# Audio tower block on one core: score sums of the first group moved to TensorE, folded bias in one matmul, other orders

## The chip, the cores and the metric

The program runs on one core of a Trainium2 chip. The metric is the device time of one execution in microseconds. Everything is in float32, or in float32r halves that together hold a float32.

## What is computed

64 signals of 750 samples are cut into 10 overlapping patches (positions) each; a patch is embedded, then one attention block and one feed-forward block follow, each behind a layer norm and with a residual:

```python
idx = arange(0, 750 - 128 + 1, 64)[:, None] + arange(128)       # 10 patches
h = einsum('bnp,dp->bnd', patches, W_tok) + b_tok               # 512 dims
z = layernorm(h); q, k, v = z @ Wq.T, z @ Wk.T, z @ Wv.T        # 16 heads of 32
q, k = rope(q, k)
s = q @ k.T / sqrt(32), causal
heavy = the key with the largest sum of softmax(s) over the queries
p = softmax(s where |i - j| <= 1 or j is heavy)  # causal mask kept
h = h + (p @ v) @ Wo.T
h = h + (silu(z2 @ Wg.T) * (z2 @ Wu.T)) @ Wd.T                  # z2 = layernorm(h), 2048 inner
```

The shape reaching the attention is 64 batches x 10 positions; the attention's sequence is the position, so its score matrices are 10 x 10 for each batch and head.

## The kernel before, in words

640 tokens lie in five tiles of 128 (`QUADRANTS`: four positions of 32 batches each). For attention the batches are in two groups of 32. Within a group a partition is one batch and one of four quarters of the heads (`NQ`), so each partition holds 4 heads x 32 dims = 128 values of a position, and scores are sums over 32 neighbouring values of a row.

Front part, in order on each engine (each engine's order is written out by hand; semaphores tie them):

- TensorE (`block.tensor`, L840 on) embeds the tokens (`embed_tokens` L847, `embed_bias` L851), folds each projection weight with the token weight (`fold_weight`, L886: main part L890, bias L896), and projects patches straight to k, q, v (`project`, L900): matmuls of 32 columns into four partition quarters at once (L912), then the folded bias is added by two identity matmuls, one for its high half (L917) and one for its low half (L919). `spread_scale` (L921) spreads the norm's reciprocal roots. Eighteen projections: for each group k, q, v in parts of 4, 4 and 2 positions.
- VectorE makes the norms (`statistics`, `token_scale`), rotates k and q of the first group out of PSUM (`rotate`), multiplies q row i with keys 0..i (`key_products`, L228) and sums over 32 dims (`scores`, L630); POOL makes the products of rows 5, 7 and 9. Then come softmax (`softmax_in` L637, `softmax_out` L652, with ScalarE's `exponential` between), `heavy_keys` (L664), the mask, a second softmax in two parts, and the value products (`values`, L232; POOL has queries 9 and 8).
- TensorE sums value products over keys by accumulating transposes (`value_sums`, L947), which also turns them; `project_out` (L955) applies Wo, and `transposes` (L935) turns the normalised tile. ScalarE evicts: `embedded`, `folded`, `folded_bias`, `drain`, `hi_attn`, `whole_tokens`.

The feed-forward runs in two passes over 16 blocks of inner dims. The first pass (token tiles 0 and 1, `gate_up_whole` L1013, `down_whole` L1023) begins as soon as these tiles are normalised; the second group's attention runs beside it on VectorE, POOL and ScalarE, an item or two between the products of two blocks (`first_pass`, L761, L463, L1030). The second pass (tiles 2 to 4, `mm3` L204) starts near 185 us. Block i's `down_whole(i - 1)` on TensorE needs VectorE's product of block i - 1 (`gu_prod`), and a block's buffers are shared by two blocks, so an engine that is late by more than a block stops the others.

SP issues all loads: patches, token weights, dims, bias, k weights, constants, q, v and o weights, then the blocks in four slots.

## Time and profile before

| | |
|---|---|
| median of 3 runs | 300.07 us (299.58 to 300.21) |
| profiled execution, own time | 299.39 us |
| its span | 297.2 us |
| TensorE busy | 270.3 us, 91% |
| VectorE busy | 160.2 us, 54% |
| ScalarE busy | 79.3 us, 27% |
| POOL busy | 63.2 us, 21% |
| mean granted clock of TensorE | 0.975 |

The page cuts the span into 40 slices of 7.4 us and prints the busy share of each in tenths:

```profile
PE   3999999418966999999999999999999999999994
DVE  0774887999789496483710535443443333433323
PEclk9999999857999999999999999999999999999999
```

A 9 is 90% or more. TensorE has weak slices at the start and from the eighth to the thirteenth; in the ninth and tenth the granted clock (1.0 is 2.4 GHz) is low too. PE is TensorE's matmuls, PEld its weight loads, DVE VectorE, ACT ScalarE, POOL GpSimd; `issue` is time in which an engine waited for nothing that the profile shows. Busy time is an average over stages with different limits, so the rows further down are read by stage and by time.

### The profile page before, as it was taken

The page shows a single profiled execution, that of the slowest core. Times are in us where ns is not written, and L with a number is a line of the kernel's source. Part 1 is how long each engine was busy: PE and PEld are TensorE (multiplying, and loading weights), DVE is VectorE, ACT ScalarE, POOL GpSimd, SP SyncE. Part 2 cuts the span into 40 slices and gives each one's busy share as a digit, 9 for nine tenths or more (in the row PEclk, how much of TensorE's full clock was granted, in tenths as well). Part 3 has the DMA queues.
Part 4 walks back from the last instruction along what each step waited for, and adds up shares of the span by engine and source line. Part 5 has one row for each costly group of instructions (what it writes and reads, how often), then busy time and mean ns, then how long its engine had stood idle before and what let it go on. Part 6 is the DMA issues. An engine that isn't in the chain of part 4 may idle for free.

```text
span 297.2 us, 4447 instructions
## 1 busy us (share of the span) xinstructions
PE 270.3 (91%) x1715; PEld 209.7 (71%) x1715; DVE 160.2 (54%) x307; ACT 79.3 (27%) x145; POOL 63.2 (21%) x47
## 2 busy tenths in 40 slices
PE   3999999418966999999999999999999999999994
PEld 1555566216455787676786567789999999999993
DVE  0774887999789496483710535443443333433323
ACT  1322053020411010325010202334443334434320
POOL 0124065000241500003600000123233222233210
PEclk9999999857999999999999999999999999999999
DMA  7971130000000353353340321548423244330003
GB/s 236 426 327 46 63 108 4 0 0 0 3 0 1 106 205 105 116 176 144 131 187 2 106 89 25 191 141 306 169 106 106 106 146 154 124 106 0 0 0 106
DMA packets 6814, 32.44 MB, mean 109 GB/s; under 512 B 976, under 2 KB 976, under 8 KB 6288
## 3 DMA queue, kind: packets, MB, share of 16 engines
q1 hardware_dynamic: 6512, 31.85, 30.6%
q10 hardware_dynamic: 288, 0.39, 0.4%
q8 instruction: 10, 0.16, 0.2%
q14 instruction: 4, 0.03, 0.0%
HBM read 30.93 MB, written 1.31 MB: 108 GB/s over the span
## 4 chain that ended last, share of the span: by engine, by line
PE 77%; issue 10%; DVE 6%; POOL 4%; DMA 1%; ACT 0%; SPq 0%; DVEq 0%; POOLq 0%
PE ps L204 34%; PE ps L1013 16%; PE ps L1023 9%; PE ps L890 4%; PE ps L955 3%; PE ps L947 3%; PE ps L847 2%; POOL prod L228 2%; PE ps L912 2%; DVE prod L228 1%; DMA wtok<-w_tok 1%; DVE by_sin L593 1%; PE ps L896 1%; DVE sm L630 1%; POOL prod L232 1%
## 5 line engine op out<-in xcount | busy, mean ns | idle before, releaser
L204 PE MATMUL ps<-xT,wgu 128*128 128x384 f32 x384 | 70.9, 340 | 0.1
L204 PEld LDWEIGHTS ps<-xT,wgu 128*128 128x128 f32 x384 | 68.1, 188 | 2.5 <-DVE xT L571 0.9
L1013 PE MATMUL ps<-whole,stage 128*128 128x256 f32 (+1 forms) x288 | 58.3, 357 | 1.4 <-ACT whole L368 1.4
L1013 PEld LDWEIGHTS ps<-whole,stage 128*128 128x128 f32 x288 | 49.6, 190 | 12.2 <-issue 3.6
L758 DVE TENSOR_TENSOR gu<-silu,ps 128x256 f32<-128x256 f32 (+1 forms) x32 | 15.5, 486 | 78.3 <-PE ps L204 44.5
L297 POOL TENSOR_TENSOR wd<-stage,wd 128x512 fp32r<-128x512 f32 x16 | 27.1, 1692 | 78.4 <-ACT wd L368 78.4
L461 ACT ACTIVATE silu<-ps 128x256 f32<-128x256 f32 (+1 forms) x32 | 14.0, 437 | 85.0 <-PE ps L1013 58.6
L204 PE MATMUL ps<-wd,hT 128*128 128x512 f32 x144 | 35.7, 393 | 0.0
L1023 PE MATMUL ps<-stage,gu 128*128 128x512 f32 x64 | 30.1, 593 | 2.9 <-DVE gu L758 2.9
L204 PEld LDWEIGHTS ps<-wd,hT 128*128 128x128 f32 x144 | 26.8, 188 | 5.0
L368 ACT ACTIVATE wgu<-stage 128x1024 fp32r<-128x1024 f32 x16 | 16.9, 1058 | 22.9 <-PE ps L204 20.9
L303 POOL TENSOR_TENSOR rs<-var,neghalf 128x1 f32<-128x1 f32 x10 | 5.5, 550 | 76.0 <-DVE var L543 76.0
L232 POOL TENSOR_TENSOR prod<-v_all,pr 128x1152 f32<-128x1152 f32 (+3 forms) x5 | 12.8, 2583 | 38.7 <-DVE pr L658 36.1
L747 DVE TENSOR_TENSOR wgu<-stage,wgu 128x1024 fp32r<-128x1024 f32 x16 | 19.8, 1234 | 0.7 <-ACT wgu L368 0.7
L1023 PEld LDWEIGHTS ps<-stage,gu 128*128 128x128 f32 x64 | 12.0, 190 | 11.4 <-issue 10.7
L955 PE MATMUL ps<-wo,whole 128*128 128x512 f32 x40 | 18.1, 596 | 1.5 <-issue 1.5
L630 DVE TENSOR_REDUCE sm<-prod 128x4 f32<-128x128 f32 (+9 forms) x20 | 17.6, 887 | 2.8 <-POOL prod L228 2.3
L769 DVE TENSOR_TENSOR hT<-gu,hT 128x384 fp32r<-128x384 f32 x16 | 8.9, 558 | 15.6 <-ACT hT L368 15.6
L912 PE MATMUL ps<-fold,pat 128*32 128x128 f32 x480 | 16.8, 276 | 0.0
L947 PEld LDWEIGHTS ps<-const,prod 128*128 128x128 f32 x110 | 13.7, 153 | 3.8 <-issue 3.8
L947 PE MATMUL ps<-const,prod 128*128 128x128 f32 x110 | 14.4, 292 | 1.6 <-DVE prod L232 1.6
L228 POOL TENSOR_TENSOR prod<-q_all,k_all 128x768 f32<-128x768 f32 (+2 forms) x5 | 13.0, 2610 | 12.3 <-DVE q_all L622 7.8
(94 smaller groups left out, 246.2 us busy)
## 6 DMA issues: line engine op xcount, KB each, us to landing
stage<-w_ffn SPq DMA_DIRECT2D x32, 768.0 KB, 4.3
stage<-w_k SPq DMA_DIRECT2D x1, 1024.0 KB, 7.0
stage<-w_q SPq DMA_DIRECT2D x1, 1024.0 KB, 9.7
stage<-w_v SPq DMA_DIRECT2D x1, 1024.0 KB, 11.7
wo<-w_o SPq DMA_DIRECT2D x1, 1024.0 KB, 13.7
out<-ob SPq DMA_DIRECT2D x14, 64.0 KB, 2.5
const<-consts SPq DMA_DIRECT2D x1, 505.0 KB, 7.6
out<-ob ACTq DMA_DIRECT2D x6, 64.0 KB, 1.9
```

Source lines behind the costliest of these rows:

```text
L204: ins = pe.matmul(dst, lhs[a], rhs[b], start=first and n == 0, stop=last and n == 2)
L228: return eng.tensor_tensor(products(i), repeated(q_all[:, g, i], 1, i + 1), k_all[:, g, 0:i + 1], ALU.mult)
L232: return eng.tensor_tensor(products(i).rearrange("p j (h d) -> p j h d", d=HD), v_all[:, g, 0:i + 1].rearrange("p j (h d) -> p j h d", d=H ...
L297: pool.tensor_tensor(dst, src, f32(hi), ALU.subtract).then_inc(done, 1)
L368: act.activation(dst, src, ACT.Copy).then_inc(done, 1)
L630: dve.tensor_reduce(sm[:, i, :, 0:i + 1].rearrange("p h j -> p j h"), products(i).rearrange("p j (h d) -> p j h d", d=HD), AX_X, ALU.add). ...
L747: dve.tensor_tensor(wgu[:, ring, 1], stage[:, slot, 0:2 * KT * P], f32(wgu[:, ring, 0]), ALU.subtract)\
L912: pe.matmul(ps[GB * q:GB * (q + 1), bank, DH * (i - a):DH * (i - a + 1)], pat[:, col:col + GB], fold[:, x, DH * q:DH * (q + 1)], start=i = ...
L947: ins = pe.matmul(dst, products(i)[:, j], cut["ident"], start=j == 0, stop=j == i, is_transpose=True)
L955: ins = pe.matmul(ps[:, WO_BANK[t], :], attn[:, k, P * t:P * (t + 1)], wo[:, k], start=k == 0, stop=k == KT - 1)
L1013: ins = pe.matmul(ps[:, bank, at + a:at + b], stage[:, slot, w:w + P], xf[:, k, a:b], start=k == 0, stop=k == KT - 1)
L1023: ins = pe.matmul(ps[:, DOWN[A][u], :], gu[:, i % 2, P * u:P * (u + 1)], stage[:, i % SLOTS, 2 * KT * P:FW], start=i == 0, stop=last)
```

## The change

- Score sums of the first group: VectorE makes all ten key products (`early_products`). For rows 0 to 8 TensorE sums over the 32 dims: one transposing matmul for each dim, reading every 32nd value of the products, all accumulated in one place (`score_sums`; chunks of rows 0 to 6 and 7 to 8, 112 and 68 results on the partitions). ScalarE copies them (`chunk_out`), one matmul with a 0/1 table puts each at its row, head and key on every partition of its batch (`score_place`), and VectorE takes the minimum with a causal table into `sm` (`place`). Row 9 is still reduced by VectorE. The first softmax is in two parts.
- Folded bias: half of the 32 equal rows of the bias hold its high half, the other half of them its low half (three ScalarE passes and one POOL addition), so one matmul with a table of 1/16 adds both.
- TensorE runs eight matmuls on the constant tile before the data are there; three token matmuls go ahead of their biases; tokens 3 and 4 are embedded behind the first group's q projections; `spread_scale(1)` goes behind both output projections.
- Norms 3 and 4 of the first layer norm move behind the first group's values on VectorE. POOL's value products 9 and 8 wait for the second group's first two turns and not for the norms. VectorE keeps one turn of the second group ahead of the first pass and takes the others, and four score rows, between its blocks.
- ScalarE's exponentials of the first softmax go ahead of nine drains; the last three drains go behind the first tile's eviction.
- The constants grow from 1010 to 1600 values on each partition (505 to 800 KB), and the token bias is loaded ahead of `dims`.

PSUM banks are dealt out anew to fit (most of that is left out below, as are semaphores and buffers).

```diff
-CUTS = {"ident": P, "cos": NPOS * HD, "sin": NPOS * HD, "band": NPOS * NPOS, "rank": NPOS, "batch": P, "quad": NQ}
+CUTS = {"ident": P, "cos": NPOS * HD, "sin": NPOS * HD, "band": NPOS * NPOS, "rank": NPOS, "batch": P, "quad": NQ,
+        "causal": NPOS * NPOS, "quarter": P, "low": 1, "sign": 1, "place": 9 * HQ * NPOS}
...
+CHUNKS = [(0, 7), (7, 9)]
...
-POOL_SCORES = [(0, 5), (0, 7), (0, 9), (1, 5), (1, 7)]
+POOL_SCORES = [(1, 5), (1, 7)]
 POOL_VALUES = [(0, 9), (0, 8), (1, 8), (1, 7), (1, 4)]
-SOFTMAX = [(0, 0, (0, 10)), (0, 1, (0, 8)), (0, 1, (8, 10)),
+SOFTMAX = [(0, 0, (0, 7)), (0, 0, (7, 10)), (0, 1, (0, 8)), (0, 1, (8, 10)),
            (1, 0, (0, 10)), (1, 1, (0, 10))]
...
+            sp.dma_start(bias_raw[:, :], b_tok.broadcast_to([2 * BR, D])).then_inc(dma_bias, 16)
             sp.dma_start(dims[:, :, :].rearrange("p k n -> p (k n)"), w_dims).then_inc(dma_dims, 16)
-            sp.dma_start(bias_raw[:, :], b_tok.broadcast_to([2 * BR, D])).then_inc(dma_bias, 16)
...
-            def bias_lo(x):
-                pool.wait_ge(fold_bias_hi, x + 1)
-                low(fold_lo[:, x], fold_bias[:, x], fold_hi[:, x], fold_bias_lo)
+            def bias_sum(x):
+                pool.wait_ge(fold_bias_parts, x + 1)
+                pool.tensor_tensor(fold_bias[:, x], fold_part[:, x], fold_less[:, x], ALU.add).then_inc(fold_bias_set, 1)
...
-                pool.wait_ge(score_sum, NPOS * g + i + 1)
...
             pool.wait_ge(neghalf_set, 1)
             for n in range(3):
                 power(n)
-            bias_lo(0)
+            bias_sum(0)
             key_add(0)
             key_add(1)
             key_add(2)
+            bias_sum(1)
+            bias_sum(2)
             power(3)
-            bias_lo(1)
-            bias_lo(2)
-            scores(0, 5)
-            scores(0, 7)
-            scores(0, 9)
             power(4)
             power(LN2[1])
-            pool.wait_ge(xn_ready, LN2[1] + 1 - NT)
+            power(LN2[0])
+            pool.wait_ge(turned, 2)
             values(0, 9)
-            power(LN2[0])
-            pool.wait_ge(xn_ready, LN2[0] + 1 - NT)
             values(0, 8)
             scores(1, 5)
...
             def folded_bias(x):
                 act.wait_ge(fold_bias_mm, x + 1)
-                act.activation(fold_bias[:, x], ps[:, BIAS_BANK, 0:DH], ACT.Copy).then_inc(fold_bias_sb, 1)
-                act.wait_ge(fold_bias_sb, x + 1)
-                split_hi(fold_hi[:, x], fold_bias[:, x], fold_bias_hi)
+                bank = ps[:, BIAS_BANK, 0:DH]
+                split_hi(fold_hi[:, x], bank, fold_bias_hi)
+                act.activation(fold_part[:, x], bank, ACT.Copy, scale=cut["low"]).then_inc(fold_bias_read, 1)
+                act.wait_ge(fold_bias_hi, x + 1)
+                act.activation(fold_less[:, x], f32(fold_hi[:, x]), ACT.Copy, scale=cut["sign"]).then_inc(fold_bias_parts, 1)
+            def chunk_out(n):
+                a, b = CHUNKS[n]
+                rows = HQ * (b * (b + 1) - a * (a + 1)) // 2
+                act.wait_ge(chunk_mm, n + 1)
+                act.activation(sums[0:rows, n], ps[0:rows, CHUNK_BANK[n], 0:P], ACT.Copy).then_inc(chunk_sb, 1)
...
-            split_hi(identr[:, :], cut["ident"], identr_set)
+            split_hi(quarter[:, :], cut["quarter"], quarter_set)
             folded(0)
             folded_bias(0)
-            embedded(3)
             folded(1)
             folded_bias(1)
+            embedded(3)
             embedded(4)
             folded(2)
             folded_bias(2)
+            chunk_out(0)
+            chunk_out(1)
+            for n in range(2):
+                exponential(n)
             for item in DRAIN[:9]:
                 drain(item)
-            exponential(0)
-            exponential(1)
-            exponential(2)
+            for n in range(2, 4):
+                exponential(n)
             act.wait_ge(neghalf_set, 1)
             act.activation(warm[:, :], neghalf[:, :], ACT.Silu)
             hi_attn(0)
             hi_attn(1)
-            for item in DRAIN[9:]:
-                drain(item)
             whole_tokens(1)
+            drain(("v", 1, 0))
+            drain(("v", 1, 1))
+            drain(("v", 1, 2))
             whole_tokens(0)
...
+            def score_reduce(i):
+                return dve.tensor_reduce(sm[:, i, :, 0:i + 1].rearrange("p h j -> p j h"),
+                                         products(i).rearrange("p j (h d) -> p j h d", d=HD), AX_X, ALU.add)
+            def early_products(i):
+                rotated(dve, 0, i)
+                key_products(dve, 0, i).then_inc(product_set, 1)
+            def place(n):
+                a, b = CHUNKS[n]
+                dve.wait_ge(place_mm, n + 1)
...
             rotate("k", 0)
             rotate("k", 1)
             rotate("k", 2)
-            statistics(3)
-            token_scale(3)
             rotate("q", 0)
             for i in range(4):
-                scores(0, i)
+                early_products(i)
             rotate("q", 1)
             for i in range(4, 8):
-                scores(0, i)
+                early_products(i)
             rotate("q", 2)
-            scores(0, 8)
-            scores(0, 9)
+            early_products(8)
+            early_products(9)
+            place(0)
             softmax_in(0)
+            dve.wait_ge(product_set, NPOS)
+            step(score_reduce(9))
+            place(1)
+            softmax_in(1)
+            softmax_out(0)
+            softmax_out(1)
+            heavy_keys()
+            softmax_in(2)
+            softmax_in(3)
+            softmax_out(2)
+            values(0, 7, 6)
+            softmax_out(3)
+            values(0, 5, 4, 3, 2, 1, 0)
+            statistics(3)
             statistics(4)
-            softmax_out(0)
-            heavy_keys()
-            softmax_in(1)
-            softmax_in(2)
+            token_scale(3)
             token_scale(4)
-            softmax_out(1)
-            values(0, 7, 6)
-            softmax_out(2)
-            values(0, 5, 4, 3, 2, 1, 0)
-            tables(1)
-            turn("k", 0)
             statistics(LN2[1])
             normalise(LN2[1])
-            turn("q", 0)
+            tables(1)
             statistics(LN2[0])
             normalise(LN2[0])
-            turn("k", 1)
+            turn("k", 0)
             def lo_gu(i, ring, slot):
                 dve.wait_ge(wgu_hi, i + 1)
...
                 dve.tensor_tensor(ob[:, u], ps[:, DOWN[p][u], :], h[:, FIRST[p] + u], ALU.add).then_inc(out_sb[p], 1)
-            for i in range(4):
-                scores(1, i)
             first_pass(0)
+            turn("q", 0)
             first_pass(1)
+            turn("k", 1)
+            scores(1, 0)
+            scores(1, 1)
+            first_pass(2)
+            scores(1, 2)
+            scores(1, 3)
             turn("q", 1)
-            first_pass(2)
+            first_pass(3)
             scores(1, 4)
             scores(1, 5)
             scores(1, 6)
-            first_pass(3)
+            first_pass(4)
             turn("k", 2)
             turn("q", 2)
             scores(1, 7)
-            first_pass(4)
+            first_pass(5)
             scores(1, 8)
+            first_pass(6)
             scores(1, 9)
-            first_pass(5)
-            softmax_in(3)
-            first_pass(6)
-            softmax_out(3)
+            softmax_in(4)
+            first_pass(7)
+            softmax_out(4)
             heavy_keys()
-            first_pass(7)
-            softmax_in(4)
             first_pass(8)
-            softmax_out(4)
+            softmax_in(5)
             first_pass(9)
-            values(1, 9, 6)
+            softmax_out(5)
+            values(1, 9)
             first_pass(10)
-            values(1, 5, 3)
+            values(1, 6, 5, 3)
             first_pass(11)
             values(1, 2, 1, 0)
             first_pass(12)
...
                         pe.matmul(ps[GB * q:GB * (q + 1), bank, DH * (i - a):DH * (i - a + 1)], pat[:, col:col + GB],
                                   fold[:, x, DH * q:DH * (q + 1)], start=i == a, stop=False)
                 dst = ps[:, bank, 0:DH * (b - a)].rearrange("p (i n) -> p i n", n=DH)
-                pe.wait_ge(identr_set, 1)
-                pe.wait_ge(fold_bias_hi, x + 1)
-                pe.matmul(dst, identr[:, :], repeated(fold_hi[:, x], 1, b - a), start=False, stop=False)
-                pe.wait_ge(fold_bias_lo, x + 1)
-                pe.matmul(dst, identr[:, :], repeated(fold_lo[:, x], 1, b - a), start=False, stop=True).then_inc(project_mm, 1)
+                pe.wait_ge(quarter_set, 1)
+                pe.wait_ge(fold_bias_set, x + 1)
+                pe.matmul(dst, quarter[:, :], repeated(fold_bias[:, x], 1, b - a), start=False, stop=True).then_inc(project_mm, 1)
+            def score_sums(n, last):
+                a, b = CHUNKS[n]
+                rows = HQ * (b * (b + 1) - a * (a + 1)) // 2
+                pairs = prod[:, a * (a + 1) // 2:b * (b + 1) // 2].rearrange("p j (h d) -> p (j h) d", d=HD)
+                read_out(*last)
+                pe.wait_ge(product_set, b)
+                for d in range(HD):
+                    ins = pe.matmul(ps[0:rows, CHUNK_BANK[n], 0:P], pairs[:, :, d], cut["ident"],
+                                    is_transpose=True, start=d == 0, stop=d == HD - 1)
+                ins.then_inc(chunk_mm, 1)
+            def score_place(n, last):
+                a, b = CHUNKS[n]
+                rows = HQ * (b * (b + 1) - a * (a + 1)) // 2
+                read_out(*last)
+                pe.wait_ge(chunk_sb, n + 1)
+                pe.matmul(ps[:, SCORE_BANK[n], 0:HQ * NPOS * (b - a)], sums[0:rows, n],
+                          cut["place"][0:rows, HQ * NPOS * a:HQ * NPOS * b], start=True, stop=True).then_inc(place_mm, 1)
             def spread_scale(g):
...
                 project(("k", 0, n), ("embedding", 0))
             read_out("fold", 0)
             fold_weight(1)
-            embed(4)
-            project(("q", 0, 0), ("embedding", 3))
+            project(("q", 0, 0), ("fold", 0))
             project(("q", 0, 1), ("scale", 0))
-            project(("q", 0, 2), ("embedding", 4))
+            project(("q", 0, 2), ("embedding", 2))
+            embed(3, ("projection", ("k", 0, 0)))
+            embed(4, ("projection", ("k", 0, 1)))
             read_out("fold", 1)
             fold_weight(2)
-            for n in range(3):
-                project(("v", 0, n), ("projection", ("k", 0, n)))
-            read_out("fold", 2)
+            score_sums(0, ("embedding", 3))
+            score_place(0, ("embedding", 4))
+            score_sums(1, ("projection", ("q", 0, 0)))
+            score_place(1, ("projection", ("q", 0, 1)))
+            project(("v", 0, 0), ("projection", ("k", 0, 2)))
+            project(("v", 0, 1), ("chunk", 0))
+            project(("v", 0, 2), ("projection", ("q", 0, 2)))
             project(("k", 1, 0), ("fold", 2))
-            project(("k", 1, 1), ("projection", ("q", 0, 0)))
-            project(("k", 1, 2), ("projection", ("v", 0, 0)))
-            project(("q", 1, 0), ("projection", ("q", 0, 1)))
-            project(("q", 1, 1), ("projection", ("v", 0, 1)))
-            project(("q", 1, 2), ("projection", ("v", 0, 2)))
-            project(("v", 1, 0), ("projection", ("q", 0, 2)))
+            project(("k", 1, 1), ("chunk", 1))
+            project(("k", 1, 2), ("scores", 0))
+            project(("q", 1, 0), ("scores", 1))
+            project(("q", 1, 1), ("projection", ("v", 0, 0)))
+            project(("q", 1, 2), ("projection", ("v", 0, 1)))
+            project(("v", 1, 0), ("projection", ("v", 0, 2)))
             project(("v", 1, 1), ("fold bias", 2))
             project(("v", 1, 2), ("projection", ("k", 1, 0)))
-            read_out("projection", ("q", 1, 2))
+            value_sums(0, ("projection", ("q", 1, 0)))
+            project_out(1, 1, ("projection", ("k", 1, 1)))
+            value_sums(1, ("projection", ("k", 1, 2)))
+            project_out(0, 2, ("projection", ("q", 1, 2)))
+            read_out("projection", ("q", 1, 1))
             pe.wait_ge(apart_set, NT)
             spread_scale(1)
-            value_sums(0, ("projection", ("q", 1, 0)))
-            project_out(1, 1, ("projection", ("k", 1, 1)))
...
+              "causal": np.tile(np.where(pos[None, :] <= pos[:, None], BIG, -BIG).reshape(-1), (P, 1)),
+              "quarter": (lane[:, None] // GB == lane[None, :] // GB) / f(GB // 2),
+              "low": (lane[:, None] % GB >= GB // 2), "sign": np.where(lane[:, None] % GB < GB // 2, 1, -1)}
+    place = np.zeros((P, 9, HQ, NPOS), dtype=f)
+    for a, b in CHUNKS:
+        for row, (i, j, n) in enumerate((i, j, n) for i in range(a, b) for j in range(i + 1) for n in range(HQ)):
+            place[row, i, n, j] = 1
+    tables["place"] = place.reshape(P, -1)
```

## Rows read from the trace of the kernel before

**Rows 1.** Stages: start:end, length, busy us (and count) of PE, PEld, DVE, ACT, POOL, then PEclk, DMA, GB/s
```profile
10.00:20.00 10.00, 10.00 (x84) 4.67 (x83) 7.64 (x26) 3.66 (x8) 2.11 (x4) 1.00 1.01 423
50.00:60.00 10.00, 5.01 (x98) 3.19 (x88) 8.05 (x18) 1.21 (x3) 2.62 (x2) 0.84 0.01 2
60.00:70.00 10.00, 3.58 (x17) 3.56 (x18) 9.32 (x25) 2.22 (x4) 0.00 (x0) 0.50 0.00 0
```
**Rows 2.** Timeline at 87 and 96 us: start, length, engine, line, operation, idle before
```profile
87.28 0.55 DVE L559 TENSOR_SCALAR xn<-h,mv,rstd 128x512 f32<-128x512 f32 x1
...
95.98 1.96 PE L1023 MATMUL ps<-stage,gu 128*128 128x512 f32 x4 [2.90 <-DVE gu L758]
```
**Rows 3.** Timeline of TensorE, token matmuls of the first 20 us
```profile
4.56 3.75 PE L847 MATMUL ps<-wtok,pat 128*128 128x512 f32 x4 [4.56 <-DMA wtok<-w_tok]
...
16.55 1.12 PE L847 MATMUL ps<-wtok,pat 128*128 128x512 f32 x2
```
**Rows 4.** Timeline of VectorE, from the first to the last instruction of three norms
```profile
10.92 0.69 DVE L540 BATCH_NORM_STATS2 stats<-h 128x6 f32<-128x512 f32 x1 [0.23 <-ACT h L372]
...
16.82 0.23 DVE L565 TENSOR_SCALAR apart<-const,rstd 128x4 f32<-128x4 f32 x1
```
**Rows 5.** Chain that ended last: start, length, what; first projection, q fold, first q projection
```profile
18.42 1.01 PE ps L912 x32
19.43 0.43 PE ps L917
19.86 0.23 PE ps L919
...
22.78 3.43 PE ps L890 x8
26.21 1.01 PE ps L896 x32
...
30.37 1.01 PE ps L912 x32
```
**Rows 6.** Timeline of POOL at 28 us: low half of the folded q bias
```profile
27.98 0.45 POOL L297 TENSOR_TENSOR fold_lo<-fold_bias,fold_hi 128x128 fp32r<-128x128 f32 x1 [2.27 <-ACT fold_hi L368]
```
**Rows 7.** Costliest groups (count, busy us, mean ns, idle before) and timeline of VectorE at 52 us
```profile
L630 DVE TENSOR_REDUCE sm<-prod 128x4 f32<-128x128 f32 (+9 forms) x20 | 17.6, 887 | 2.8 <-POOL prod L228 2.3
...
52.10 1.49 DVE L630 TENSOR_REDUCE sm<-prod 128x40 f32<-128x1280 f32 x1 [1.43 <-POOL prod L228]
```
**Rows 8.** Groups by line from 130 to 185 us: transposing matmuls and their weight loads
```profile
L947 PE MATMUL ps<-const,prod 128*128 128x128 f32 x55 | 6.3, 273 | 0.0
L947 PEld LDWEIGHTS ps<-const,prod 128*128 128x128 f32 x55 | 6.1, 141 | 1.1 <-issue 1.1
```
**Rows 9.** Timeline of VectorE: a reduction in order, one with a step, a 320-element operation
```profile
56.26 0.57 DVE L656 TENSOR_REDUCE rowv<-pr 128x40 f32<-128x400 f32 x1
...
57.91 0.93 DVE L667 TENSOR_REDUCE hvy<-pr 128x40 f32<-128x400 f32 x1
...
60.46 0.49 DVE L681 TENSOR_TENSOR keep<-hvy,const 128x320 f32<-128x320 f32 x1
```
**Rows 10.** Timeline of values, value sums and first output projection
```profile
66.03 2.23 DVE L232 TENSOR_TENSOR prod<-v_all,pr 128x1024 f32<-128x1024 f32 x2
...
67.40 4.53 PE L947 MATMUL ps<-const,prod 128*128 128x128 f32 x26 [1.65 <-DVE prod L232]
...
72.67 3.67 PE L955 MATMUL ps<-wo,whole 128*128 128x512 f32 x8 [0.73 <-issue]
```
**Rows 11.** Stages around 70 us, columns as in Rows 1
```profile
66.00:70.00 4.00, 2.60 (x13) 2.63 (x14) 3.90 (x7) 0.00 (x0) 0.00 (x0) 0.50 0.00 0
...
71.00:72.00 1.00, 0.93 (x9) 0.70 (x7) 1.00 (x4) 0.03 (x1) 0.00 (x0) 1.00 0.00 0
```
**Rows 12.** Timeline at 80 us: POOL and VectorE at once
```profile
80.12 2.79 POOL L232 TENSOR_TENSOR prod<-v_all,pr 128x1280 f32<-128x1280 f32 x1 [1.29 <-DVE xn L559]
...
80.56 2.97 DVE L593 TENSOR_TENSOR by_sin<-q_all,tsin 128x256 f32<-128x256 f32 x2
```

67 lines of the change are left out of this document (37 added, 30 removed).

## The prediction

> **What bounds the kernel now.** I read the busy time of each engine by stage first [rows 1]. From 50 to 60 us TensorE works 5.0 of 10 us, from 60 to 70 only 3.6; VectorE works 8.1 and 9.3 there. The page's slices then show TensorE nearly full from 96 us to the end. Then I followed the chain that ended last to the point where that full part begins: the first down projection, `down_whole(0)`, at 95.98 us, which had itself waited 2.90 us for a product of VectorE [rows 2]. From there TensorE alone sets the time, so what the change earns is how far that instruction moves forward, less the stalls that it puts behind it. Everything before it is a relay between TensorE (folds, projections) and VectorE (rotations, scores, softmax, values), so I walk the new order through both engines with the durations of the old trace.
>
> **The start.** TensorE waits until 4.56 us for data; its first four 512-column passes take 3.75 us, two later ones 1.12 us [rows 3]. So it starts at about half pace, the lower of its two clocks (1.2 of 2.4 GHz), and rises later. Eight warm-up matmuls are 16 passes of 128 columns, a quarter of those: 0.23 us each, 3.6 us from 1.45 us, until 5.1. That delays the embedding by 0.55 us and takes 1.65 off it. With the mean at the full clock too, the first eviction starts some 0.7 us earlier. Then VectorE needs 16.82 + 0.23 - 10.92 = 6.1 us for three norms [rows 4], which no longer hides behind `embed(3)`: the first projection starts at about 16.6 us where it stood at 18.42 [rows 5]. That is 1.8 us of gain; TensorE alone, without this wait, would give 3.3. The bias transfer moves ahead of `dims`, which TensorE then wants at 7.2 us: 0 to 0.4 us, taken as 0, since a 128 KB transfer is all that is put in front. The constants grow by 295 KB ahead of the q and v weights; at 423 GB/s [rows 1] that is 0.7 us, for weights wanted 6 us after they land: nothing, and 0.7 at most if that cover were gone.
>
> **Folded bias in one matmul.** The second bias matmul costs 0.23 us of a 1.67 us projection [rows 5], 0.12 in a half-width one, so a set of three falls from 4.36 to 3.77 us and six sets give 3.5 us. But `embed(4)` no longer stands between a fold and its projection. Fold and bias take 3.43 + 1.01 us [rows 5] and end at 16.6 + 3.8 + 4.4 = 24.8. Before, the low half was ready 1.2 us behind that (27.98 + 0.45 against 27.22) [rows 5, 6]; with one more ScalarE pass of 0.3 it is ready at 26.3, while the four-way matmuls end at 25.8: a new wait of 0.5 us. The first q projection is done at 26.75 (30.37 before [rows 5]), the third at 29.1. Two embeddings of 1.5 us each and the v fold follow: TensorE is free at 36.5.
>
> **Score sums.** Line 630's reductions take 17.6 us for two groups, 8.8 for the first; only the last of them (1.49) stays, so 7.3 us go. Products that POOL made (with 1.43 us of waiting behind the last) come back to VectorE [rows 7], at the price of a reduction of equal size. VectorE so has three q rotations (5.4) and ten products (8.8) from 26.75: until 40.95. TensorE starts summing seven score rows at 36.5. A transposing matmul takes 6.3/55 = 0.115 us [rows 8]: 32 are 3.7, copy 0.3, 0/1 matmul 0.55, so 41.1, level with VectorE. The second chunk runs beside VectorE's softmax input and last reduction and is placed at 45.5. Placing costs as a 320-element operation, 0.49 us [rows 9]. Softmax of both parts takes 3.1 us more, heavy keys 2.55 (57.91 to 60.46 [rows 9]): done at 51.2; masks and softmax input at 54.5.
>
> Here a new wait decides. ScalarE's queue holds nine drains ahead of the masked exponentials, and they need three projection sets: 45.5 + 3 x 3.77 = 56.8, drain 0.4, exponential 0.5. VectorE, ready at 54.5, waits 3 us with all of the values queued behind. The values start at 59.2 against 66.03 [rows 10]: 6.8 us gained.
>
> What no row shows is the read. All transposes of this trace read 128 neighbouring elements; the new ones read every 32nd element, 112 or 68 of them. Low bound: 0 more. High bound, from VectorE: the same 400 elements are reduced in 0.57 us in order and in 0.93 us with a step [rows 9], 0.9 ns an element more, so 0.1 us for each of the first 32 and almost nothing for the shorter 32: 3.4 us. It would lie on the path in full, as TensorE feeds both the placing and the drains. One row is the same engine, the other the same pattern; neither is clearly nearer, so I take the middle, 1.7 us.
>
> The Trainium skill (SBUF - State Buffer, Door 1: The DMA port swizzle, the note on cachelines) says that reads which leave their 16-byte line each time pay a penalty. The stepped reduction agrees. By that rule the sum would come to the upper bound, without it to the lower.
>
> **Behind the values.** From 66.03 to the output projection at 72.67 are 6.6 us, with 26 transposes in 4.53 [rows 10], partly at half clock [rows 11]. TensorE now comes straight from the v projections, without the ten idle microseconds (waiting for the fifth token scale) in which the clock fell: 1.1 us less, so it projects at 64.8. Both output projections are done at 73.8, 8.1 us ahead. The two deferred norms cost VectorE 4.0 us ahead of the first residual, 65.3 to 69.3; the first projection is done at 68.4, so 0.9 of them is exposed, and it is made good: normalised tile 1 is out at 73.0, before TensorE has time for it. Then `tables(1)` waits for the scale matmul at 74.2, and tile 0 is out at 79.0, where it was 87.83 [rows 2]. TensorE does transposes, gate and up of tile 1 until 79.2 and those of tile 0 until 84.2. VectorE's product is ready by then, because one turn stands ahead of it and not three turns with four score rows. So 84.2 against 95.98: 11.8 us.
>
> **Load moved behind the start.** Two turns (4.2) and four score rows (3.7) of the second group now run beside the first passes of 5.2 us each, and POOL's two products of the first group's values run there back to back. One such product of 2.79 us stretched a VectorE pair to 2.97 from 0.75 [rows 12]: 2.2 us each, 5 in all. By the same walk the third product of the pass ends 0.3 us after TensorE wants it and the fifth 0.4 after: 0.7 us lost. The others have 1 to 3 us of room. Between 0 and 3; I take 0.7. Sum: -11.8 + 0.7 + 1.7 = -9.4 us. The profiled execution took 299.39 us (span 297.2 and 2.2 around it), the median of the runs 300.07; less 9.4 that is 290.0 and 290.7.
>
> **Rivals.** (1) *Transposes into one place don't overlap.* Place: the two score sums. If each waited for its load and its predecessor, 0.141 + 0.273 us [rows 8] in place of 0.115, 64 of them add 19.1: -11.1 + 19.1 = +8, 308 us, slower. It decides from 0.115 + 11.1/64 = 0.29 us each. Against it: value sums accumulate up to ten into one place at 0.115. 5 in 100. (2) *VectorE becomes the bound of the passes.* Softmax and the lock with POOL come 4 to 5 us later against TensorE than I count, and the products of passes 4, 7 and 9 hold it: 294 to 297 us. For it: 12 us of work are moved there; against it: VectorE waited in most of these passes before. 11 in 100. (3) *The change doesn't do what it says*: ScalarE's order and the new waits for bank reads give the gain back, and TensorE's 8 us of added matmuls stay: 299 to 301. 5 in 100. (4) *The clock falls in the score sums.* 64 cold transposes at 2.60/13 = 0.20 us [rows 11] add 5.4, the projections behind them 1.7: 298. Against it: the clock went from 0.50 to 1.00 by 71 us while TensorE did transposes alone [rows 11]. 3 in 100. The Trainium skill (TensorE: Matmul & The Clock Gate, Part 4) says that transposes don't count as busy for the clock; by that rule this rival would hold, and the trace disagrees.
>
> **How the numbers follow.** The forecast has 76 in 100, with 288 to 293.5 by the two bounds of the read and those of the stalls. The range reaches a little lower for a start without the 0.55 us delay, and up to 296 to take in most of rival 2 and a clock that falls in the new 1.7 us gap at 15 us (1.7). Faster by over 0.2% (about what this measurement can tell from no change) 0.90; within 0.2% 0.04; slower 0.06.
>
> **What would show it.** The first projection at 16.6; a 0.5 us wait for the q bias; 32 strided transposes in 3.7 us (low bound) or 6.9 (high); VectorE waiting for the masked exponential until about 57.5; no half clock after 10 us; `down_whole(0)` between 84 and 88 and no hole over 1 us behind it. The prediction is wrong if a score sum takes over 7 us, if VectorE's products hold the passes by more than 3 us, or if TensorE's idle time before `down_whole(0)` only changes place.

## The result, and the profile after

The changed kernel takes 288.94 us (median of 4 runs, 288.47 to 289.57) against 299.82 beside it: a ratio of 0.962 [0.958, 0.966], 10.9 us less. The forecast was 290.7, a gain of 9.4. The profiled execution took 288.86 us, its span 286.9 (297.2 before). TensorE is busy 274.6 us of it (96%), though it has more to do than before. The forecast had taken 288 to 293.5 as its range.

Executions of one kernel often split in two groups by mean granted clock, and the mean of those at 0.995 or more is called "at full clock" below; it is 288.47 us for the changed kernel in its second set of runs.

The page's slices (7.2 us each, tenths) of the changed kernel:

```profile
PE   7979999998899999999999999999999999999994
DVE  2582987779669998696904435463333334333323
PEclk9999999999999999999999999999999999999999
```

The hollow from the eighth to the thirteenth slice is gone, and with it the low clock in it. By stage (start:end, length, busy us and count of PE, PEld, DVE, ACT and POOL, then the granted clock, the busy share of the DMA engines and their GB/s, as in [rows 1]):

```profile
30.00:40.00 10.00, 10.00 (x70) 5.61 (x70) 9.72 (x17) 2.62 (x6) 0.64 (x1) 1.00 0.13 35
40.00:50.00 10.00, 9.09 (x129) 7.51 (x128) 7.55 (x17) 2.62 (x10) 0.00 (x0) 1.00 0.11 46
50.00:60.00 10.00, 10.00 (x228) 6.86 (x224) 6.54 (x22) 5.97 (x15) 0.00 (x0) 1.00 0.01 3
60.00:70.00 10.00, 8.72 (x73) 5.41 (x66) 9.48 (x24) 1.11 (x3) 1.10 (x2) 1.00 0.01 2
```

From 50 to 60 us TensorE now never stops and VectorE has time to spare; before it was the other way round. From 60 to 70 TensorE does 8.7 us of work where it did 3.6. The walk's stations, TensorE by time (start, duration, line, operands, count, and in brackets the wait ahead of it and who ended it):

```profile
1.45 3.78 PE L1018 MATMUL ps<-average 128*128 128x128 f32 x16 [1.45 <-DVE average L720]
5.02 2.89 PE L882 MATMUL ps<-wtok,pat 128*128 128x512 f32 x4
...
17.13 0.39 PE L984 MATMUL ps<-apart,const 128*128 128x12 f32 x2 [1.75 <-DVE apart L578]
17.45 0.75 PE L951 MATMUL ps<-fold,pat 128*32 128x128 f32 x20
...
27.31 0.47 PE L956 MATMUL ps<-fold_bias,quarter 128*128 128x512 f32 x1 [0.70 <-POOL fold_bias L320]
...
37.45 3.75 PE L966 MATMUL ps<-const,prod 128*112 128x128 f32 x32
41.66 0.71 PE L976 MATMUL ps<-const,sums 112*128 112x280 f32 x2 [0.46 <-ACT sums L392]
42.21 3.66 PE L966 MATMUL ps<-const,prod 128*68 128x128 f32 x32
46.32 0.42 PE L976 MATMUL ps<-const,sums 68*128 68x80 f32 x2 [0.45 <-ACT sums L392]
...
61.76 1.90 PE L1005 MATMUL ps<-const,prod 128*128 128x128 f32 x15
64.20 1.50 PE L1005 MATMUL ps<-const,prod 128*128 128x128 f32 x11 [0.55 <-DVE prod L238]
66.43 3.67 PE L1013 MATMUL ps<-wo,whole 128*128 128x512 f32 x8 [0.73 <-issue]
...
85.85 1.88 PE L1086 MATMUL ps<-stage,gu 128*128 128x512 f32 x4
```

L1018 is the warm-up, L882 the first four token passes, L984 spreads the scales of the first norms (1.75 us without work ahead of it: the hole), L966 are the new sums, L976 the placing, L1005 the value sums, L1013 the output projection, and the first L1086 is `down_whole(0)`. It starts at 85.85 where it started at 95.98 [rows 2], and nothing waits behind it: of all 64 matmuls of that line the page says

```profile
L1086 PE MATMUL ps<-stage,gu 128*128 128x512 f32 x64 | 30.1, 592 | 0.0
```

with no idle time ahead of any. On the chain that ended last, the sums are these two pieces:

```profile
37.52 3.69 PE ps L966 x32
42.37 3.51 PE ps L966 x32
```

3.69/32 is 0.115 us for a transposing matmul with 112 columns read 128 bytes apart, the same as the transposes of neighbouring elements in [rows 8]. The read with a step costs TensorE no time here. It isn't free for the single weight load: in this trace a load of 112 columns with the step lasts 174 ns and one of 68 columns 137, where one of 128 neighbouring columns lasts 141. But the loads overlap, and the pace of the matmuls stays. And VectorE, from [rows 9, 10]:

```profile
58.88 0.49 DVE L683 TENSOR_REDUCE rowv<-pr 128x32 f32<-128x320 f32 x1 [2.81 <-ACT pr L419]
...
60.39 1.22 DVE L238 TENSOR_TENSOR prod<-v_all,pr 128x1024 f32<-128x1024 f32 x1
```

It waited 2.81 us for the masked exponential, as forecast (3), and the values started at 60.39.

### The profile page after: what moved, and what is told of

Read it like the earlier page. It is cut to its first block, busy times and chain, and to the rows that moved or that the text cites. A ratio compares the mean times of both kernels' runs of the same rounds, so it can differ in the third digit from the quotient of the medians.

```text
span 286.9 us, 4588 instructions
## 1 busy us (share of the span) xinstructions
PE 274.6 (96%) x1781; PEld 215.9 (75%) x1781; DVE 160.8 (56%) x309; ACT 80.3 (28%) x151; POOL 54.7 (19%) x44
## 4 chain that ended last, share of the span: by engine, by line
PE 91%; DVE 4%; ACT 1%; issue 1%; POOL 0%; DVEq 0%
PE ps L210 35%; PE ps L1076 20%; PE ps L1086 10%; PE ps L1013 6%; PE ps L951 4%; PE ps L1005 4%; PE ps L966 3%; PE ps L929 2%; PE ps L956 2%; PE ps L882 2%; PE ps L1018 1%; DVE prod L238 1%; PE ps L993 1%; PE ps L935 1%; DVE stats L553 1%
## 5 line engine op out<-in xcount | busy, mean ns | idle before, releaser
L1086 PE MATMUL ps<-stage,gu 128*128 128x512 f32 x64 | 30.1, 592 | 0.0
L1013 PE MATMUL ps<-wo,whole 128*128 128x512 f32 x40 | 18.1, 596 | 1.5 <-issue 1.5
L1086 PEld LDWEIGHTS ps<-stage,gu 128*128 128x128 f32 x64 | 12.0, 190 | 8.3 <-issue 7.7
L234 DVE TENSOR_TENSOR prod<-q_all,k_all 128x128 f32<-128x128 f32 (+9 forms) x18 | 17.0, 976 | 0.3
L238 DVE TENSOR_TENSOR prod<-v_all,pr 128x896 f32<-128x896 f32 (+8 forms) x15 | 15.2, 1066 | 0.2
L951 PEld LDWEIGHTS ps<-fold,pat 128*32 128x32 f32 x480 | 12.1, 109 | 3.5 <-issue 3.0
L1005 PEld LDWEIGHTS ps<-const,prod 128*128 128x128 f32 x110 | 12.2, 141 | 3.2 <-issue 2.1
## 6 DMA issues: line engine op xcount, KB each, us to landing
stage<-w_q SPq DMA_DIRECT2D x1, 1024.0 KB, 10.1
```

The lines of the kernel that those rows point to most:

```text
L234: return eng.tensor_tensor(products(i), repeated(q_all[:, g, i], 1, i + 1), k_all[:, g, 0:i + 1], ALU.mult)
L238: return eng.tensor_tensor(products(i).rearrange("p j (h d) -> p j h d", d=HD), v_all[:, g, 0:i + 1].rearrange("p j (h d) -> p j h d", d=H ...
L951: pe.matmul(ps[GB * q:GB * (q + 1), bank, DH * (i - a):DH * (i - a + 1)], pat[:, col:col + GB], fold[:, x, DH * q:DH * (q + 1)], start=i = ...
L1005: ins = pe.matmul(dst, products(i)[:, j], cut["ident"], start=j == 0, stop=j == i, is_transpose=True)
L1013: ins = pe.matmul(ps[:, WO_BANK[t], :], attn[:, k, P * t:P * (t + 1)], wo[:, k], start=k == 0, stop=k == KT - 1)
L1086: ins = pe.matmul(ps[:, DOWN[A][u], :], gu[:, i % 2, P * u:P * (u + 1)], stage[:, i % SLOTS, 2 * KT * P:FW], start=i == 0, stop=last)
```

## The experiments

Edits are against the changed kernel if nothing else is said. Times are medians; a ratio is to the kernel before, run beside. The runs fall in three groups, each on another chip: the first holds the warm-up, the first undoing of the sums, bias twice and sums twice; the second the changed kernel again, biases between, exponentials ahead and POOL back; the third the second undoing and the three with the hole filled. The changed kernel was run again in the second alone, so times are compared across groups. The kernel before allows it: its executions at a mean clock of 0.974 to 0.976 average 299.9, 299.9 and 299.7 us in the three. In the third group more of its executions had a lower clock, which makes the ratios there look some 0.4% better; go by the times.

**The changed kernel again.** No edit.

> The changed kernel once more, as the base of the three beside it, which differ from it by less than one per cent: 288.9 us.

Measured: 288.69 us, ratio 0.964 [0.960, 0.967]. Four executions took 288.1 to 288.7 us at a mean clock of 0.998 or more, two took 290.1 and 290.8 at 0.993 and 0.992. So the kernel has a loss of 2 us in it that comes in some executions; the runs below show where most of it lies. The profiled execution has a span of 286.2, 0.7 less than the first one, and all of the 0.7 comes in the first token passes:

```profile
5.02 2.15 PE L882 MATMUL ps<-wtok,pat 128*128 128x512 f32 x4
...
16.72 1.08 PE L951 MATMUL ps<-fold,pat 128*32 128x128 f32 x32
...
85.12 1.88 PE L1086 MATMUL ps<-stage,gu 128*128 128x512 f32 x4
```

The four passes took 2.15 us and not 2.89: the pace of TensorE doubles at another moment from one execution to the next, and every later station is earlier by the same 0.73. Over all profiles with the warm-up these four passes take 1.90 to 3.07 us. So stations of two runs are compared below by their distance from an earlier station.

**Without the warm-up.**

```diff
-            for n in range(8):
-                pe.matmul(ps[:, 3, 0:P], average[:, :], average[:, :], start=True, stop=True)
```

> The changed kernel without the eight warm-up matmuls. Theory (the warm-up pays, but its gain was spent on putting three token matmuls ahead of the biases): the first four token passes go from 2.89 us back to about 3.75 and start 0.5 us earlier, the clock rises during the mean; first eviction at about 11.2 us (10.31 with the warm-up), the first projection at about 18.3 (17.45), and the whole +0.6 to +0.9 us: 289.6 to 289.9. Rival (the norms wait for something else, the mean or the bias transfer): no difference, 288.9.

Measured: 291.51 us, ratio 0.972 [0.968, 0.976]; one execution of 290.80 at 0.997, three of 291.3 to 291.8 at 0.993 or 0.994. TensorE of this run:

```profile
4.88 3.75 PE L882 MATMUL ps<-wtok,pat 128*128 128x512 f32 x4 [4.88 <-DMA wtok<-w_tok]
...
18.41 0.39 PE L984 MATMUL ps<-apart,const 128*128 128x12 f32 x2 [1.75 <-DVE apart L578]
18.73 1.08 PE L951 MATMUL ps<-fold,pat 128*32 128x128 f32 x32
...
20.37 1.94 PE L951 MATMUL ps<-fold,pat 128*32 128x128 f32 x32
```

The first projection is 1.3 or 2.0 us later than in the two profiles with the warm-up, and then comes something not expected: behind the hole a projection takes 1.94 us instead of 1.08. Against the executions of the changed kernel that lose time at the same place (mean 290.43), the warm-up is worth 1.2 us (291.59 for the three here); against those at full clock, 2.3 (one execution, 290.80). Both are more than the 0.6 to 0.9 expected.

**The score sums undone.** VectorE reduces again, POOL makes rows 5, 7 and 9 again; with them the first softmax is in one part and ScalarE's nine drains are ahead of all exponentials again (left out of the cut below). The rest stays as changed.

```diff
-POOL_SCORES = [(1, 5), (1, 7)]
+POOL_SCORES = [(0, 5), (0, 7), (0, 9), (1, 5), (1, 7)]
...
-                early_products(i)
+                scores(0, i)
...
-            score_sums(0, ("embedding", 3))
-            score_place(0, ("embedding", 4))
-            score_sums(1, ("projection", ("q", 0, 0)))
-            score_place(1, ("projection", ("q", 0, 1)))
```

> The changed kernel with the first group's score sums as before: VectorE reduces all ten rows, POOL makes three products, one softmax part, ScalarE's drains ahead of all exponentials; all else stays changed. Theory (the score sums are nearly half of the gain, since VectorE's relay is shortened by its reductions and by the waits for POOL, and TensorE's 8 us of added matmuls fall into its hole): values start at about 64 us and not at 60.4, TensorE idles over 8 us ahead of them and its clock falls to half once more, +4 to +5.5 us: 293 to 294.5. Rival (TensorE's added matmuls cost what VectorE saves; the gain is in the order of norms and turns): within 1.5 us of 288.9.

Measured: 297.76 us, ratio 0.990 [0.986, 0.995], far more than either theory. Its trace says why:

```profile
47.68 1.08 PE L945 MATMUL ps<-fold,pat 128*32 128x128 f32 x16 [6.01 <-DVE by_sin L605]
...
58.47 0.57 DVE L683 TENSOR_REDUCE rowv<-pr 128x40 f32<-128x400 f32 x1 [3.19 <-ACT pr L422]
```

A v projection waited 6.01 us for a PSUM bank that VectorE read late, which made the drains late and VectorE wait 3.19 us for the exponential behind them; it also waited 3.2 us for POOL's products, the first of which stood behind the sum of the v bias. These are costs of the edit's banks and queue, not of the sums. So the run says little, and it was made anew with both mended (the first edit is against the changed kernel, the second against the run above):

```diff
-PROJECT_BANK = [1, 2, 4, 3, 5, 6, 4, 1, 6, 0, 3, 2, 5, 4, 1, 6, 7, 0]
+PROJECT_BANK = [1, 2, 4, 3, 5, 6, 1, 2, 4, 0, 3, 1, 5, 2, 4, 6, 7, 0]
...
-            bias_sum(2)
             scores(0, 5)
+            bias_sum(2)
```

> The score sums back on VectorE and POOL once more, now with the projections' banks as in the kernel before and POOL's product of row 5 ahead of its v bias sum, so that TensorE's v projections don't wait for a bank that the third q rotation reads, and ScalarE's drains are done before the first exponential. Theory (of the 9 us that the run with score sums back lost, 3.2 were that wait of VectorE behind late drains and 1 to 2 the wait for POOL; the score sums themselves are worth less): first exponential without a wait, values start at about 63.5 to 64.5 us, 293.5 to 295. Rival (the score sums themselves are worth the 9 us): 297 or more.

Measured: 292.41 us, ratio 0.972 [0.967, 0.977]. TensorE now runs through its projections and then has nothing to do:

```profile
64.26 5.01 PE L999 MATMUL ps<-const,prod 128*128 128x128 f32 x26 [10.75 <-DVE prod L238]
70.00 2.38 PE L1007 MATMUL ps<-wo,whole 128*128 128x512 f32 x5 [0.73 <-issue]
```

The 7.4 us of sums, and their placing, are gone from TensorE and turn into idle time: it waits 10.75 us for VectorE, the clock falls in the wait (5.01 us for 26 transposes, 3.00 at full clock), and the output projection stands 3.6 us later than in the changed kernel. The sums bring 292.41 - 288.7 = 3.7 us, less than the 4.8 to 6.3 expected (293.5 to 295); the rest of the 10.9 comes from elsewhere. Of the 3.6 at the output projection 2.0 are the transposes at half clock.

**The folded bias added by two matmuls**, each half of it.

```diff
-                pe.matmul(dst, quarter[:, :], repeated(fold_bias[:, x], 1, b - a), start=False, stop=True).then_inc(project_mm, 1)
+                pe.matmul(dst, quarter[:, :], repeated(fold_bias[:, x], 1, b - a), start=False, stop=False)
+                pe.matmul(dst, quarter[:, :], repeated(fold_bias[:, x], 1, b - a), start=False, stop=True).then_inc(project_mm, 1)
...
-              "quarter": (lane[:, None] // GB == lane[None, :] // GB) / f(GB // 2),
+              "quarter": (lane[:, None] // GB == lane[None, :] // GB) / f(GB),
```

> The changed kernel with each folded bias added by two matmuls of the quarter table at half its value. Theory (TensorE is the path through all 18 projections but for one short wait): 12 x 0.23 + 6 x 0.12 = 3.5 us more of TensorE, of which the q1 and v1 parts in front of the values count too: +2.8 to +3.5, 291.7 to 292.4. Rival (the projections hide behind VectorE's relay, the single bias matmul bought little): +0 to +1.2, up to 290.1.

Measured: 292.70 us, ratio 0.975 [0.969, 0.981]; at full clock 291.57, so +3.1 us against the 3.5 of pure TensorE time. The projections are on the path nearly in full.

**The sums done twice.** The result in PSUM is doubled, which changes only the numbers.

```diff
-                for d in range(HD):
+                for d in 2 * list(range(HD)):
```

> The changed kernel with each of the two score sums made twice over into the same bank, 64 more transposing matmuls of 0.115 us. Theory (both sums are on the path in full: placing, then the projections that ScalarE must drain ahead of the exponential): +7.4 us, 296.3. Rival (VectorE is level with TensorE there, so the second sum hides behind its softmax input and last reduction): +3.7 to +5 us, 292.6 to 294.

Measured: 295.65 us, ratio 0.985 [0.982, 0.988]; at full clock 295.37, +6.9 for 7.4 us of added matmuls. No slack hides the sums: TensorE, not VectorE, is the bound from the first sum to the values. A penalty for the read with a step, had there been one, would have been paid in full.

**The token biases between the token matmuls.**

```diff
             average_dims()
+            embed_bias(0)
+            embed_bias(1)
             embed_tokens(2)
-            for t in range(3):
-                embed_bias(t)
+            embed_bias(2)
```

> The changed kernel with the first two token bias matmuls put back between the mean and the third token matmul, as in the kernel before. Theory (the 1.75 us that TensorE waits for the third norm begins with the late first eviction): first eviction at 9.3 us and not 10.31, VectorE's norms start at 9.9 behind its centring, first projection at 16.4 to 16.6, -0.8 to -1.0 us: 287.9 to 288.1. Rival (the q relay ahead of the score sums has slack, TensorE only waits elsewhere): 0 to -0.3.

Measured: 287.89 us (287.15 to 289.01), ratio 0.959 [0.956, 0.962], all six executions at 0.998 or more. That is a mean of 288.0, 0.5 us less than the changed kernel at full clock: between the theory (0.8 to 1.0) and the rival (0 to 0.3). The profiled one lost the gain to a late transfer, and shows a smaller hole all the same:

```profile
8.52 1.35 PE L922 MATMUL ps<-dims,average 128*128 128x160 f32 x8 [1.53 <-DMA dims<-w_dims]
...
17.14 0.39 PE L984 MATMUL ps<-apart,const 128*128 128x12 f32 x2 [0.49 <-DVE apart L578]
```

`dims` landed 6.2 us after its issue and TensorE waited 1.53 us for it. The hole is smaller because the third pair of token passes and its bias (1.3 us) now come behind the bias with which the norms begin: 1.75 less 1.3 is about the 0.49 that is left.

**Masked exponentials ahead of three drains.**

```diff
-            for item in DRAIN[:9]:
+            for item in DRAIN[:6]:
                 drain(item)
             for n in range(2, 4):
                 exponential(n)
+            for item in DRAIN[6:9]:
+                drain(item)
```

> The changed kernel with ScalarE's two masked exponentials ahead of the last three of the nine drains. Theory (the wait of 2.81 us that VectorE has for the exponential reaches TensorE only in the value sums and first eviction, since TensorE has the v projections of group 2 until 61.8): values start 2.7 us earlier, the 0.55 us hole in the value sums goes and they end at 64.8 and not 65.7: -0.8 to -1.0 us, 288.0. Rival (the wait that my sum called decisive is on the path in full): -2.5 us or more, 286.4 or less.

Measured: 288.96 us, ratio 0.961 [0.958, 0.964]; at full clock 287.83, so -0.6, while three of six executions, at 0.990 to 0.994, took 289.5 to 289.6. The profiled one is of these. Its TensorE behind the hole, and the granted clock (third from last) by the microsecond:

```profile
17.32 0.39 PE L986 MATMUL ps<-apart,const 128*128 128x12 f32 x2 [1.75 <-DVE apart L580]
17.64 1.94 PE L953 MATMUL ps<-fold,pat 128*32 128x128 f32 x32
```

```profile
17.00:18.00 1.00, 0.69 (x10) 0.65 (x14) 0.84 (x4) 0.00 (x0) 0.00 (x0) 0.82 0.97 406
...
20.00:21.00 1.00, 1.00 (x17) 0.73 (x20) 0.60 (x1) 0.00 (x0) 0.00 (x0) 0.50 0.98 406
```

Behind the hole the clock goes from 1.00 to 0.50 (2.4 to 1.2 GHz) until 21 us, in some executions and not in others. From the spread of the scales to the first score sum this profile takes 21.85 us (17.32 to 39.17), both profiles of the changed kernel 20.3. So 1.5 of the 2 us lie here; where the rest lies isn't shown.

The 2.81 us wait of VectorE is gone and its products come sooner, but TensorE is busy with projections until the value sums anyway. From the first score sum to `down_whole(0)`, a stretch behind the fall of the clock, it takes

```profile
86.51 1.88 PE L1088 MATMUL ps<-stage,gu 128*128 128x512 f32 x4
```

86.51 - 39.17 = 47.3 us, where the changed kernel takes 85.85 - 37.45 = 48.4. So the wait was worth 1.1 us by the trace, of which 0.55 is TensorE's wait inside the value sums; by the few executions at full clock it is 0.6.

**POOL's value products where they were.** They start after the second and the first normalised tile.

```diff
-            power(LN2[0])
-            pool.wait_ge(turned, 2)
+            pool.wait_ge(xn_ready, LN2[1] + 1 - NT)
             values(0, 9)
+            power(LN2[0])
+            pool.wait_ge(xn_ready, LN2[0] + 1 - NT)
             values(0, 8)
```

> The changed kernel with POOL's two value products of the first group behind the first and second norm of the feed-forward part, as before, and not behind the second turn. Theory (they share a read path with VectorE's two-input operations, and where they stand decides who pays): product 9 runs from 74.1 beside the table products, product 8 from 81 beside the first turn; the first feed-forward product comes 1 to 2 us late and TensorE waits: +0.8 to +1.5 us, 289.7 to 290.4. Rival (the hole ahead of it takes them in): within 0.3 of 288.9.

Measured: 289.92 us, ratio 0.965 [0.961, 0.969]. One of its six executions took 467.14 us at a mean clock of 0.562; it is in this median and not in the ratio, and nothing on record says what happened in it. The median of the other five is 288.99. At full clock they take 288.69, so +0.2, within the 0.3 of the rival. VectorE in that run, while POOL makes its second product (from 80.72, 2.57 us):

```profile
81.16 2.75 DVE L607 TENSOR_TENSOR by_sin<-k_all,tsin 128x256 f32<-128x256 f32 x2
...
84.61 0.42 DVE L790 TENSOR_TENSOR gu<-silu,ps 128x256 f32<-128x256 f32 x1
```

The pair takes 2.75 instead of 0.75, but VectorE would otherwise have waited 1.98 us for ScalarE there. Its product comes 67.55 us behind the first projection (17.06), against 67.30 in the changed kernel (84.75 and 17.45): 0.25 us late, as the time says.

**The hole filled.** `embed(3)` goes ahead of the scales, where it stood before the change; `embed(4)` stays behind the q projections. The biases stand as in the changed kernel; a bank and ScalarE's eviction of the token tile move with the edit (left out below).

```diff
             fold_weight(0)
+            embed(3, ("embedding", 2))
             pe.wait_ge(apart_set, 3)
...
-            embed(3, ("projection", ("k", 0, 0)))
             embed(4, ("projection", ("k", 0, 1)))
```

> The changed kernel with the fourth token tile embedded where TensorE waits 1.75 us for the third norm, and not behind the q projections. Theory (the hole is real slack, and it is also what makes the clock fall in the first projections in about a third of the executions, which then take 1.5 to 2 us more): the hole is 0.3 us, the mean clock is 0.998 or more in all executions, projections from 17.45 as before, placing 0.7 to 1.0 us earlier: 287.7 to 288.1, and no execution over 289. Rival (VectorE's products bound the placing, and the clock falls for other reasons): 288.7 and a third of the executions with a mean clock of 0.99.

Measured: 288.59 us, ratio 0.958 [0.953, 0.963]. Five executions took 287.4 to 289.0 at 0.999 or more. A sixth took 292.8 at 0.947, which the expectation excluded; where its clock fell, no trace shows. The hole is

```profile
16.58 0.39 PE L984 MATMUL ps<-apart,const 128*128 128x12 f32 x2 [0.26 <-DVE apart L578]
```

0.26 us long, and the projections behind it run at 1.08. In time it brings 0.3 us at full clock (mean of the five 288.2), less than expected. The trace gives more:

```profile
36.09 3.72 PE L966 MATMUL ps<-const,prod 128*112 128x128 f32 x32 [0.59 <-DVE prod L234]
...
84.45 1.88 PE L1086 MATMUL ps<-stage,gu 128*128 128x512 f32 x4
```

The first score sum starts 19.5 us behind the spread of the scales (16.58) and not 20.3, so 0.8 us is gained. The embedding taken out of that stretch is 1.4 us; 0.59 of it turns into a wait for VectorE's products, as the rival said of all of it. Behind the first sum nothing changes: 84.45 - 36.09 = 48.4 us, VectorE waits 2.79 us for the exponential and TensorE 0.54 in the value sums, as before. Why the executions gain less than this profile isn't shown.

**The hole filled and the exponentials ahead.** Both edits together.

> The same with ScalarE's two masked exponentials ahead of the last three drains as well. Theory: the two gains add, since the second one fell on the value sums (the undisturbed executions of the run with exponentials ahead were 0.8 us shorter in span): 286.8 to 287.3. Rival (one hides the other): as the run with the fourth tile moved alone.

Measured: 286.98 us (286.54 to 287.43), ratio 0.953 [0.949, 0.957]: 1.5 us under the changed kernel at full clock. By their own times the parts give 0.3 and 0.6; by the traces they give 0.8 and 1.1, and here the same two stretches are as short as in the single runs:

```profile
36.20 3.72 PE L968 MATMUL ps<-const,prod 128*112 128x128 f32 x32 [0.60 <-DVE prod L234]
...
83.52 1.88 PE L1088 MATMUL ps<-stage,gu 128*128 128x512 f32 x4
```

19.5 us from the spread of the scales (16.70) to the first sum, as with the hole filled alone, and 83.52 - 36.20 = 47.3 to `down_whole(0)`, as with the exponentials ahead alone. The two gains add, as expected. Right ahead of the values and in their sums neither engine waits for the other:

```profile
56.23 2.23 DVE L238 TENSOR_TENSOR prod<-v_all,pr 128x1024 f32<-128x1024 f32 x2
```

```profile
60.37 3.00 PE L1007 MATMUL ps<-const,prod 128*128 128x128 f32 x26
```

**The same with `dims` loaded ahead of the bias again.**

```diff
-            sp.dma_start(bias_raw[:, :], b_tok.broadcast_to([2 * BR, D])).then_inc(dma_bias, 16)
             sp.dma_start(dims[:, :, :].rearrange("p k n -> p (k n)"), w_dims).then_inc(dma_dims, 16)
+            sp.dma_start(bias_raw[:, :], b_tok.broadcast_to([2 * BR, D])).then_inc(dma_bias, 16)
```

> The same again with the dims transfer ahead of the bias transfer, as in the kernel before. Theory (dims landed 4.3 to 6.2 us after its issue at 2.28 in these kernels, against 3.6 after 1.69, and TensorE waited for it for 0.25 to 1.53 us in three profiles; the bias is wanted only at 9.4): the wait for dims is gone and the first projection is at 16.8 or earlier when the clock rises early: -0.2 to -0.6 us against the kernel without this, 286.4 to 287. Rival (the bias casts then hold the first eviction): +0.3.

Measured: 286.86 us (286.62 to 287.41), ratio 0.953 [0.949, 0.957]. Against the run above it is 0.1 us, within the spread, where 0.2 to 0.6 was expected. This and the version above are the fastest here, 1.5 us ahead of the changed kernel at full clock and some 4.3% ahead of the kernel before (299.8).

## Why the prediction was right, and where it was off

*The bound and the mechanism* held. `down_whole(0)` moved from 95.98 to 85.85, TensorE never waits from there on, and the rest of the span is as long as before (286.9 - 85.85 = 201.1, against 297.2 - 95.98 = 201.2). The gain is where the walk put it. By parts: 3.7 us for the score sums, 3.1 for the single bias matmul, 1.2 to 2.3 for the warm-up. What is left by subtraction, 1.8 to 2.9 of 10.9, is put down to the other orders (embeddings, norms, turns); they were not tried one by one, and that the parts add is assumed.

*The walk to `down_whole(0)`* said 84.2, and the two profiles show 85.85 and 85.12, so -10.1 and -10.9 instead of -11.8. Its steps:

- *First projection, 16.6*: 17.45 and 16.72. The warm-up took 3.78 us (3.6 worked out). VectorE's first norm starts at 10.94 and 10.21; 10.92 less 0.7 was worked out. The step was right for an execution whose pace doubles early in the token passes, and 0.85 short for the other. That this moment moves by 0.7 us between the two, and by more over all profiles, was not in the sum.
- *Wait for the q bias, 0.5*: 0.70 in both; the first q projection is done at 27.7 and 27.0, walked 26.75.
- *The sums*: matmuls as worked out (3.69 for 32). But the hops between engines had too small a price: 0.46 and 0.45 us until ScalarE's copy is seen, where 0.3 was taken, and 0.71 for the first placing instead of 0.55. The second placing ends at 46.7 and 45.9, walked 45.5.
- *Values and output projection, 59.2 and 64.8*: the values start at 60.39 and 59.66; then TensorE waits 0.55 us in the value sums and 0.73 behind them: 66.43 and 65.71. Two hops more, 0.4 us beyond the walk.

So with the early pace the walk was 0.9 us short, with the late one 1.65, and what was mis-sized apart from the pace is hops of 0.1 to 0.2 us each.

*The read with a step* was taken at 1.7 us, the middle of 0 and 3.4, and is 0. This is the largest wrong term. Its upper bound was too low as well: it counted almost nothing for the second chunk, and by its own 0.9 ns an element the 68 columns there would add 2.0 us. With the term at 0 that changed nothing. Doubling the sums added 6.9 us for 64 matmuls, 0.108 each. The row to go by was the one of the same engine, [rows 8], not the same pattern on VectorE [rows 9]. The Trainium skill (SBUF - State Buffer, Door 1: The DMA port swizzle, the note on cachelines) has a penalty for each read that leaves its line. VectorE's reductions agree with it (0.93 against 0.57). TensorE's weight loads show a longer single load (174 ns against 141), but the time of its sums shows none.

*The stalls behind* were taken at 0.7 us and are 0. The lock between POOL and VectorE came as told:

```profile
87.24 5.02 POOL L238 TENSOR_TENSOR prod<-v_all,pr 128x1280 f32<-128x1280 f32 x2 [7.68 <-DVE q_all L635]
```

```profile
87.41 2.79 DVE L601 TENSOR_TENSOR by_cos<-k_all,tcos 128x512 f32<-128x512 f32 x1
90.13 2.74 DVE L606 TENSOR_TENSOR by_sin<-k_all,tsin 128x256 f32<-128x256 f32 x2
...
94.83 0.41 DVE L789 TENSOR_TENSOR gu<-silu,ps 128x256 f32<-128x256 f32 x1
```

Two operations of 0.68 and 0.75 took 5.5, 4.1 us more. But that product is out at 95.24 and TensorE wants it at about 96.2. The walk had it 0.3 us late. It isn't TensorE's own delay that saves it: with the hole filled and the exponentials ahead `down_whole(0)` starts at 83.52, earlier than walked, the same two operations stretch to the same 2.79 and 2.74, and no matmul behind it waits. By the span the sum is then -10.1, and 0.1 to 0.2 less behind it, -10.3; forecast were -11.8 + 0.7 + 1.7 = -9.4. Two terms too dear (1.7 and 0.7) and one too cheap (1.65) partly cancel. That the sum is nearer than its terms is luck.

*The wait for the masked exponential* was right in its size (2.81 us against 3) and wrong in its weight. It was said to decide; taking it away brought 0.6 us by the time of the executions and 1.1 by the trace, and 1.2 where the hole was filled too (288.2 to 287.0, 1.0 by the trace). TensorE's projections end at 61.8, so most of what VectorE gains finds it busy.

*The rivals.* Transposes into one place overlap (0.115). VectorE doesn't hold the passes. The gain isn't given back. The clock doesn't fall in the score sums: it is 1.00 from 30 to 50 us, and from 37.45 to 46.7 TensorE does little but the transposes of L966 (7.4 us of them). The Trainium skill (TensorE: Matmul & The Clock Gate, Part 4) says that transposes don't count as busy for the clock. The trace disagrees, as the kernel before did [rows 11]. The clock falls behind the gap at 15 us instead, which was allowed for only as an end of the range with 1.7 us. So the sign "no half clock after 10 us" holds in both profiles of the changed kernel, but by the mean clocks not in all of its executions.

*What starts that fall is open.* Of 27 executions with the full hole (1.50 to 1.75 us: the changed kernel again, bias twice, sums twice, exponentials ahead, and five of POOL back), 11 have a mean clock of 0.990 to 0.994 and take about 2 us more. Of the four of the first result one is at 0.994, and without the warm-up it is three of four. Four profiles fell on such an execution (no warm-up, bias twice, sums twice, exponentials ahead) and all show half clock right behind the hole; five others with the same hole don't. Of 24 executions of the four variants with a hole of 0.26 to 0.49 us, one is below 0.995, the one at 0.947. That speaks for the hole. Against it as the only cause: the kernel before, whose TensorE has no hole there, also has executions of two kinds, 20 of 35 at a mean clock of 0.974 to 0.976 and 15 at 0.966 to 0.971, and the second kind takes 2.0 us more. Its profile is of the first kind, so no trace shows where those lose.

## What to carry to other kernels

An order that takes work away from a wait leaves a hole there. Ask what else could stand in it: the same embedding put back earned 0.8 us by the trace, and the fall of the clock was seen in none of the four profiles with the hole filled or shortened. A wait is worth what reaches the engine that bounds: VectorE's 2.8 us were worth 1.1. Where executions scatter by more than the effect, distances between stations of the trace tell what medians of six can't: by medians the two last edits seemed to help each other, by the stations they simply add. A price for a read is best taken from the same engine. An undoing of one part must have its banks and queues laid out anew, or it measures these: 297.8 us and 292.4 were two undoings of the same thing.
